# Layer 1's dense weights of a four-layer graph network are turned through memory instead of by TensorE

## The reference

```
def _weighted_mean_agg(ft, w, src, dst, n_nodes):
    m = ft[src] * w[:, None]
    msum = jax.ops.segment_sum(m, dst, num_segments=n_nodes)
    wsum = jax.ops.segment_sum(w, dst, num_segments=n_nodes)
    ...
neigh1 = _weighted_mean_agg(feat, w, src, dst, n)
neigh2 = _weighted_mean_agg(feat, w, dst, src, n)
```

## Time and profile before

| what | value |
|---|---|
| median of 3 runs | 9473.14 us (9472.91 to 9473.69) |
| time of the profiled execution | 9470.78 us |
| its span, first to last instruction | 9469.0 us |
| mean granted TensorE clock | 0.978 of full speed |
| PE, DVE, ACT, POOL busy over the span | 91%, 62%, 61%, 57% |

### The profile page before, as it was taken

How to read it: one execution, slowest core, us unless ns; L and a number is a source line. 1 busy time by engine, 2 the same in 40 slices (tenths; PEclk the granted TensorE clock), 3 DMA queues, 4 the chain that set the end, 5 groups by cost and what they waited for, 6 DMA issues and landing times. The chain is left out here.

```text
span 9469.0 us, 228933 instructions
## 1 busy us (share of the span) xinstructions
PE 8637.6 (91%) x58595; PEld 6939.6 (73%) x58596; DVE 5874.3 (62%) x12349; ACT 5795.2 (61%) x15455; POOL 5415.5 (57%) x5229
## 2 busy tenths in 40 slices
PE   5999999999998899999988888888885899999998
PEld 5999999999997677775656666666654666666666
DVE  7777777787876677762125555555554555555555
ACT  5888888888885544440016677677763555555555
POOL 5777777777773000000005777777771677777775
PEclk7999999999999999999999999999998999999999
DMA  3111111111111122225544444444430222222222
GB/s 129 45 44 44 44 44 44 45 44 44 44 44 48 69 109 115 115 95 191 191 140 142 118 118 118 118 118 118 118 112 33 77 73 73 73 73 73 73 73 69
DMA packets 463488, 819.24 MB, mean 87 GB/s; under 512 B 160570, under 2 KB 330610, under 8 KB 443634
## 3 DMA queue, kind: packets, MB, share of 16 engines
q0 software_dynamic: 193536, 455.41, 16.6%
q1 hardware_dynamic: 269810, 362.04, 11.0%
HBM read 668.94 MB, written 147.98 MB: 86 GB/s over the span
## 5 line engine op out<-in xcount | busy, mean ns | idle before, releaser
L1776 POOL DMA_INDIRECT x<-table,p_gidx x1632 | 1542.4, 945 | 2375.3 <-ACT p_gidx L1813 1968.7
L618 POOL DMA_INDIRECT g_G<-table,g_runs x1776 | 2146.9, 1209 | 549.0 <-issue 538.8
L2228 POOL DMA_INDIRECT c_G<-table,c_gidx x1632 | 1543.7, 946 | 505.2 <-issue 497.0
L757 PE MATMUL g_ps_cell<-g_kw,g_loh 128*128 128x98 f32 x9472 | 1224.4, 273 | 28.6 <-DVE g_kw L675 28.6
L757 PEld LDWEIGHTS g_ps_cell<-g_kw,g_loh 128*128 128x128 f32 x9472 | 1154.6, 193 | 28.8 <-DVE g_kw L675 28.8
L1866 PE MATMUL p_ps_sum<-x 128*96 128x256 f32 x3264 | 898.5, 399 | 232.1 <-DVE hid L1802 223.1
L768 PE MATMUL g_ps_rev<-g_hrow,g_AT 128*128 128x129 f32 x7252 | 1047.6, 281 | 66.0 <-ACT g_AT L734 66.0
L768 PEld LDWEIGHTS g_ps_rev<-g_hrow,g_AT 128*128 128x128 f32 x7252 | 903.9, 192 | 94.0 <-ACT g_AT L734 94.0
L1866 PEld LDWEIGHTS p_ps_sum<-x 128*96 128x96 f32 x3264 | 469.0, 163 | 647.0 <-ACT x L1831 272.5
L1802 DVE TENSOR_TENSOR hid<-hid,p_ps_sum 96x256 f32 x1632 | 677.1, 415 | 363.8 <-DVE hid L1802 360.5
L1338 ACT CAST a_A<-a_ps_cell 128x392 bf16<-128x392 f32 x1184 | 510.8, 492 | 541.8 <-PE a_ps_cell L1372 541.8
(11 more groups left out here) (345 smaller groups left out, 16644.2 us busy)
## 6 DMA issues: line engine op xcount, KB each, us to landing
adj_save<-a_A SPq DMA_DIRECT2D x74, 1568.0 KB, 5.1
a_A<-adj_save SPq DMA_DIRECT2D x74, 1568.0 KB, 6.5
c_ed<-in_edge_dram SPq DMA_DIRECT2D x1632, 25.0 KB
g_G<-table,g_runs POOLq DMA_INDIRECT x1776
p_lhs<-in_edge_dram SPq DMA_DIRECT2D x1632, 16.0 KB
x<-table,p_gidx POOLq DMA_INDIRECT x1632
c_G<-table,c_gidx POOLq DMA_INDIRECT x1632
table<-m_rows SPq DMA_DIRECT2D x17, 384.0 KB
```

The lines of the kernel that those rows point to most:

```text
L618: g.indirect_dma_start(G[:, e % GR, q, 0:D], None, table, bass.IndirectOffsetOnAxis(ap=runs[:, n % 2, 0, RQ * e + q:RQ * e + q + 1], axis= ...
L757: last = pe.matmul(ps_cell[q % 2][:, r * KEYS:(r + 1) * KEYS], loh[:, b, cell, :], kw[:, b, cell, :], start=True, stop=True)
L1776: g.indirect_dma_start(G[:, H * b + q, :], None, table2, bass.IndirectOffsetOnAxis(ap=gidx[:, b, q:q + 1], axis=0)).then_inc(gathered[b], 16)
L2228: g.indirect_dma_start(G[:, H * b + q, :], None, table, bass.IndirectOffsetOnAxis(ap=gidx[:, b, q:q + 1], axis=0)).then_inc(gathered[b], 16)
```

## The change

The product of a cell is formed the other way round (`kw` is now the weight operand, `loh` the moving one), so it comes out as 98 keys on partitions x 128. ScalarE copies four of them into one of eight slots of `X`. SP stores each slot to a buffer in memory (`turn_save`, 392 pieces of 512 bytes, 16 stores a batch) and loads it back in four transfers a batch, each into 32 partitions of `AT` (25,088 bytes a partition), which then holds all 49 turned tiles of a batch in two buffers. `turn`, its PSUM banks and ScalarE's copies from them are gone. Keys are numbered differently in this stage (`number`), so that a slot's 49 tiles are contiguous in memory. The backward products of a batch come five steps later (`LATE`). The body of SP's program is now the body of a batch: first the load of `runs`, then the 16 stores with the loads of turned tiles between them. `slots` (a small table of the list stage) is laid out the other way round.

```diff
+LATE = 5
+XR = 8
+QT_HALVES = 4
+QUARTERS = HALVES // QT_HALVES
+QSLOTS = P // QUARTERS
...
+    turn_save = dram("turn_save", (2, HALF, KEYS, P), F32)
...
-                A = sb("g_A", [P, 2, KEYS, HALF], F32, ctx)
-                AT = sb("g_AT", [P, 2, TG * P], F32, ctx)
+                X = sb("g_X", [P, XR, CQ * P], F32, ctx)
+                AT = sb("g_AT", [P, 2, BUCKETS * P], F32, ctx)
...
-                    return [(-2, TGS - 2), (-2, TGS - 1)] if s == 0 else [(-1, s - 1)]
+                    if s < LATE:
+                        return [(-2, TGS - 2 - LATE + s)]
+                    return [(-2, TGS - 2), (-2, TGS - 1)] if s == LATE else [(-1, s - 1 - LATE)]
...
-                        def load(i, bb):
-                            n = 2 * i + bb
+                        def load_runs(n, bb):
+
                             if not (isinstance(n, int) and n < 2):
                                 sp.wait_ge(weighted, RPB * (n - 1))
                             sp.dma_start(runs[:, bb, :, :], run_save[:, :, bass.ds(n * RD, RD)]).then_inc(runs_in[bb], 16)
 
-                        over_batches(sp, load)
+                        def store(n, bb, q):
+
+                            sp.wait_ge(evacd, HALVES * n + q + 3)
+                            sp.dma_start(turn_save[bb, CQ * q:CQ * (q + 1), :, :].rearrange("c k l -> k c l"),
+                                         X[0:KEYS, q % XR, :].rearrange("k (c l) -> k c l", c=CQ)).then_inc(stored[q // QT_HALVES], 16)
+
+                        def load_turned(m, b, z):
+
+                            sp.wait_ge(stored[z], 16 * QT_HALVES * (m + 1))
+                            sp.dma_start(AT[QSLOTS * z:QSLOTS * (z + 1), b, :],
+                                         turn_save[b, HALF // QUARTERS * z:HALF // QUARTERS * (z + 1), :, :].rearrange("c (j h) l -> (c j) (h l)", j=GRP)
+                                         ).then_inc(turned[b], 16)
+
+                        def body(i, bb):
+                            n = 2 * i + bb
+                            if known(n):
+                                load_runs(n, bb)
+                                if known(n - 2):
+                                    sp.wait_ge(turned[bb], 16 * QUARTERS * i)
+                            for q in range(HALVES):
+                                if known(n):
+                                    store(n, bb, q)
+                                if q == 1 and known(n - 1):
+                                    load_turned(n - 1, 1 - bb, QUARTERS - 1)
+                                if known(n) and q == 9:
+                                    if known(n - 2):
+                                        sp.wait_ge(rev_made, TGS * (n - 1))
+                                    load_turned(n, bb, 0)
+                                    load_turned(n, bb, 1)
+                                if known(n) and q == 13:
+                                    load_turned(n, bb, 2)
+
+                        over_bodies(sp, body)
...
-                        g.iota(number[:, :, :], [[1, KEYS], [0, CQ]], 1, 0, allow_small_or_imprecise_dtypes=True).then_inc(consts, 1)
+                        g.iota(number[:, :, :], [[1, GRP], [GRP, BUCKETS], [0, CQ]], 1, 0, allow_small_or_imprecise_dtypes=True).then_inc(consts, 1)
...
+                                    if q % QT_HALVES == 0:
+                                        z = q // QT_HALVES
+                                        if z >= 2:
+                                            s.wait_ge(stored[z - 2], 16 * QT_HALVES * (n + 1))
+                                        elif known(n - 1):
+                                            s.wait_ge(stored[z + 2], 16 * QT_HALVES * n)
                                     s.wait_ge(built, HALVES * n + q + 1 + 2 * NOH0)
-                                    if q == 0 and known(n - 2):
-                                        s.wait_ge(applied, n - 1)
-                                    s.copy(A[:, bb, :, q * CQ:(q + 1) * CQ], ps_cell[q % 2][:, 0:CQ * KEYS].rearrange("p (c k) -> p k c", k=KEYS)).then_inc(evacd, 1)
-                                m = n - 1
-                                if known(m):
-                                    for k in (q,) if q < HALVES - 1 else (q, q + 1):
-                                        g = TGS * m + k
-                                        w = len(tiles_of(k)) * P
-                                        b = (1 - bb + k) % 2
-                                        s.wait_ge(turned, g + 1)
-                                        s.copy(AT[:, b, 0:w], ps_turn[b][:, 0:w]).then_inc(at_ready, 1)
+                                    s.copy(X[0:KEYS, q % XR, :], ps_cell[q % 2][0:KEYS, :]).then_inc(evacd, 1)
...
-                                last = pe.matmul(ps_cell[q % 2][:, r * KEYS:(r + 1) * KEYS], loh[:, b, cell, :], kw[:, b, cell, :], start=True, stop=True)
+                                last = pe.matmul(ps_cell[q % 2][0:KEYS, r * P:(r + 1) * P], kw[:, b, cell, :], loh[:, b, cell, :], start=True, stop=True)
...
                         def backward(m, b, i, k):
 
                             g = TGS * m + k
-                            pe.wait_ge(at_ready, g + 3)
                             pe.wait_ge(rev_added, g + 1)
                             if k == 0:
+                                pe.wait_ge(turned[b], 16 * QUARTERS * (i + 1))
                                 pe.wait_ge(gathered[b], 16 * (i + 1))
-                            for t in range(len(tiles_of(k))):
-                                last = pe.matmul(ps_rev[(b + k) % 2][:, t * (D + 1):(t + 1) * (D + 1)], AT[:, (b + k) % 2, t * P:(t + 1) * P],
+                            for t, hi in enumerate(tiles_of(k)):
+                                last = pe.matmul(ps_rev[(b + k) % 2][:, t * (D + 1):(t + 1) * (D + 1)], AT[:, b, hi * P:(hi + 1) * P],
                                                  hrow[:, b, :], start=True, stop=True)
                             last.then_inc(rev_made, 1)
...
-                        def turn(m, b, k):
-
-                            g = TGS * m + k
-                            if k == 0:
-                                pe.wait_ge(evacd, HALVES * (m + 1) + 2)
-                            pe.wait_ge(at_ready, g + 1)
-                            for t, hi in enumerate(tiles_of(k)):
-                                last = pe.transpose(ps_turn[(b + k) % 2][:, t * P:(t + 1) * P],
-                                                    A[:, b, GRP * hi:GRP * (hi + 1), :].rearrange("p j c -> p (j c)"), ident[:, :])
-                            last.then_inc(turned, 1)
```

19 lines of the change are left out of this document (7 added, 12 removed).

## The result

The changed kernel takes 10,454.12 us (median of the four executions that count, 10,450.76 to 10,471.33; that of all six is 10,463.94) against 9,472.52 us before (6 runs): ratio 1.104, 95% interval 1.102 to 1.106. The other two took 14.5 and 20.1 ms at a lower granted clock and are left out. Forecast were 9,936 us, 9,740 to 10,126: the sign is right, the time lies outside. The profiled execution took 10,456.54 us, of which the span is 10,454.8.

The account below looks back on a forecast made before the run. The prediction took POOL (GpSimd), as well as TensorE, to bound the kernel. Terms of 43.3 us plus 1.0 gave 44.3 us a batch, 6.3 more than 37.96, 463 us on 73 batches: 9,936 us, range 9,740 to 10,126.

Parts of the forecast that it names:

- The bound of the kernel before: In the stage, POOL (GpSimd) without slack beside TensorE: 25 gathers of 1.52 us make 37.9 us a batch.
- The ring through the load of `runs`: In SP's program that load follows step 15's store, closing a chain through POOL and ScalarE: 43.3 us a batch.
- Scaling, copy, SP, load of `runs`, landing: Chain between two batches' gathers: 1.28, 0.5, 0.74, 2.47 us, and 2.15 for the last gather's landing.
- GpSimd's 30.7 + 5.5: On POOL, 25 gathers a batch at 30.7 us, plus 5.5 us of delays by VectorE's table instructions.
- For both I add 1.0: New transfers in the DMA queues, third turned-tile load and a 196 KB store, add 1.0 us a batch.
- the return trip: From the last gathers' landing to the next first gather: scaling 1.28, copy 0.5, SP 0.74, load 2.47 us.
- Slower still: Rival: TensorE late behind POOL or at half clock, 46.5 to 49 us a batch, 10,095 to 10,280 us; chance 0.11.
- What would make it wrong: Signs in the profile after: POOL without waits for `runs`, gathers near 0.94 us, or TensorE waiting for turned tiles.

Follow-up runs that it names:

- early_runs_b: The changed kernel with the load of `runs` issued one batch earlier, the transfers of turned tiles being the same: 9,485.87 us, ratio 1.0014.
- before_late_b: The kernel before, with SP's load of `runs` also waiting for ScalarE's last copy of the batch before: 9,920.34 us, ratio 1.0477.
- small_loads_b: The changed kernel with loads of turned tiles cut to one tile in 49, stores and late load of `runs` kept: 9,823.3 us, ratio 1.038.

## Why the prediction was wrong

- **The bound of the kernel before.** Right: GpSimd has no slack, and in early_runs_b the time returns when that alone is restored.
- **The ring through the load of `runs`.** Right: it makes 450 us by itself in the kernel before (before_late_b) and 353 in the changed kernel without the loads (small_loads_b), against 43.3 - 37.96 = 5.3 us a batch or 390 us by my terms; the first of the two has other parts (4.03 us in place of 2.15 up to the last scaling). The order at SP and ScalarE was as told.
- **Scaling, copy, SP, load of `runs`, landing.** Right where nothing is in the way: 1.93 and 4.94 us in small_loads_b for 2.15 and 4.99.
- **GpSimd's 30.7 + 5.5.** 36.2 forecast, 35.3 in the changed kernel, 0.9 too much. That VectorE's two-input operations hold gathers up is now shown (1.218 to 1.001 us with one of them away). The Trainium skill's page "SBUF — State Buffer", section "Who interferes with whom", infers the contrary for descriptor generation; for these gathers the measurement decides against that inference. It agrees with the same section's other sentence, on a GpSimd instruction that reads SBUF: the gathers take their row numbers from `runs`.
- **"For both I add 1.0".** This term failed, what the new transfers cost the two small ones. It measured 7.48 - 2.15 = 5.3 us for the last gather's landing and 8.54 - 4.99 = 3.6 us for the return trip, 8.9 where I took 1.0 and allowed 4.1 at the most (2.2 at the high end of the range). With the 0.9 above this is 51.3 us, and (51.44 - 37.96) x 73 = 984 on 9,473 makes 10,457. Three things were wrong in it. I looked at what was issued last, load 3 at step 13, and not at the backlog: loads 1 and 2, issued behind the store of step 9, start to move 4.2 us before the last gather's end and take 9.4 us. Load 3 had to wait for stores that drained behind them, 258.8 / 43 = 6.0 us a batch, so it fell into the return trip, right ahead of the load of `runs`. And I priced a load of 784 KB as half of one of 1,568 KB, though it has pieces twice as long into a quarter of the partitions. The Trainium skill's page "SBUF — State Buffer", section "Door 1: The DMA port swizzle", says that DMA bandwidth goes by how many of the 16 SBUF ports the partitions reach, and by its table 32 partitions reach eight. The trace agrees: 13.6 GB/s an engine against 22.6 and 23.3 with all 128, at the same bytes.
- **"Slower still".** The time is above this rival's range as well, and its mechanism is not the one. TensorE's clock does fall at its stops (windows of the changed kernel: before a stop, behind that stop of 2.9 us, and over the next one of 12.4 us and the restart at 2049.28):

```profile
2017.00:2027.00 10.00, 9.48 (x84) 9.08 (x82) 8.78 (x16) 6.77 (x18) 3.38 (x3) 1.00 0.94 203
2029.00:2033.00 4.00, 3.46 (x16) 3.46 (x17) 0.51 (x2) 0.95 (x3) 0.00 (x0) 0.57 0.98 214
2040.00:2053.00 13.00, 3.71 (x17) 3.72 (x18) 0.00 (x0) 3.56 (x10) 9.84 (x11) 0.50 0.64 142
```

It is granted 1.00, then 0.57 in the mean, and 0.50, which is the lower of its two levels (1.2 of 2.4 GHz). But the ring waits for no product of TensorE in these places, and the three terms above make the whole 51.3 us.
- **What would make it wrong.** I named TensorE waiting for turned tiles as the sign of bandwidth. That sign stayed away, and the loads were the cause nevertheless: they cost through transfers of 36 and 64 KB that share engines with them.

## What to carry to other kernels

When an edit adds bulk transfers, list every small transfer on whose landing an engine waits, and price each with the bulk pieces that are queued and still moving at that moment, not with an idle landing. Issue what a chain waits for early: the load of `runs` one batch ahead was worth 948 us here, moving one bulk load behind it 204. Load over all 128 partitions: the same bytes took 0.69 of the DMA engines' time for 0.86. And when an edit changes an engine's program inside a loop, look whether transfers of instructions appear.

## What the runs showed of the hardware

- The same bytes to SBUF at 13.6 GB/s an engine in 25,088-byte pieces for 32 partitions, and 23 in 12.5 KB pieces for 128. The length of a piece is not the reason: in the changed kernel's own trace a load of 3,328 KB (`x` from `x_save`, issued at 8085.5 us) moves 128 pieces of 26,624 bytes, one for each partition, at 26 GB/s an engine. Nor is it the traffic beside it, which is there with the shorter pieces too. Of the differences looked at, the number of partitions is left.
- Nine-microsecond stops of VectorE once in its loop, each with transfers of the instruction queue inside it, 3.6 to 4.1 us long where the loads of turned tiles are gone or reshaped. The Trainium skill's page "DMA: Bandwidth & Descriptors", section "Queues, rings and completion order", lists refills, in its row 14, among the queues on the same 16 engines; the trace agrees, these transfers are on its queue 14. In early_runs_b VectorE stands for up to 9.0 us at the same instruction, with such a transfer inside only one of 35 waits over 3 us; the profile puts that down to TensorE, and nothing is lost, as GpSimd sets the pace there.
- Eight one-input comparisons of 128 elements take 1.66 us for a table that takes 1.22 as one two-input operation, but hold GpSimd up less (1.076 us a gather for 1.218).
- Two of five chips ran the kernel before in 12.1 and 12.3 ms. Why TensorE's granted clock is lower there was not tried.
